# Chunk 1's sublayer ahead of chunk 0's ranks in the second FFN, and the rows of ones written in the first FFN

## What is computed

```python
def ffn(x):                 # top 2 of 8 experts, unweighted
    gamma = softmax(x @ w_router.T + b_router)
    mask = top_k(gamma, 2)  # as a 0/1 mask over 8 experts
    return einsum('bte,bteo->bto', mask, x @ w_experts.T + b_experts)
def attn(t):                # causal, 16 heads, scale 1/4
    out = softmax_causal(q @ k.T / 4) @ v
    x = out @ w_proj + b_proj + t
    return layernorm(x) * ln_gamma + ln_beta
x = x + 0.5 * ffn(ln(x))
x = x + attn(ln(x))
x = x + 0.5 * ffn(ln(x))
```

## Time and profile before

| | us |
|---|---|
| median of 3 runs | 1021.81 (1019.46 to 1022.9) |
| profiled execution, its own time | 1021.86 |
| its span, first to last instruction | 1020.1 |
| PE busy | 966.9 (95%) |
| DVE busy | 833.7 (82%) |
| ACT busy | 512.4 (50%) |
| POOL busy | 264.5 (26%) |
| granted PE clock, mean | 0.974 of 2.4 GHz |

### The profile page before, as it was taken

How to read it: one execution, slowest core, us unless ns; L and a number is a source line. 1 busy time by engine, 2 the same in 40 slices (tenths; PEclk the granted TensorE clock), 3 DMA queues, 4 the chain that set the end, 5 groups by cost and what they waited for, 6 DMA issues and landing times.

```text
span 1020.1 us, 18105 instructions
## 1 busy us (share of the span) xinstructions
PE 966.9 (95%) x5602; PEld 575.7 (56%) x5602; DVE 833.7 (82%) x2444; ACT 512.4 (50%) x1053; POOL 264.5 (26%) x289
## 2 busy tenths in 40 slices
PE   6899999999888699999999999999998899999997
PEld 5678887888665233333333333333344677777776
DVE  5677776767675999999999999999767788888775
ACT  4225434442322277777777777777774333232310
POOL 1012202221420412222122121221342443434211
PEclk9999999999996699999999999999999899999999
DMA  6201101113113412222222223322320111110001
GB/s 224 83 1 63 63 0 62 63 41 84 62 43 82 126 40 66 75 68 72 70 70 72 75 76 75 76 75 76 95 54 13 43 63 63 62 56 21 7 21 41
DMA packets 55058, 64.27 MB, mean 63 GB/s; under 512 B 13776, under 2 KB 37312, under 8 KB 54976
## 3 DMA queue, kind: packets, MB, share of 16 engines
q1 hardware_dynamic: 54384, 62.47, 21.5%
q10 hardware_dynamic: 592, 0.80, 0.2%
HBM read 41.30 MB, written 21.23 MB: 61 GB/s over the span
## 4 chain that ended last, share of the span: by engine, by line
PE 86%; DVE 8%; issue 2%; ACT 2%; DMA 1%; POOL 1%; DVEq 0%; SPq 0%; POOLq 0%; ACTq 0%
PE bank L354 39%; PE bank L1503 14%; PE bank L1330 14%; PE bank L1487 13%; PE bank L800 2%; PE bank L346 2%; DMA v_all<-L_ffn_w_experts 1%; ACT b_probs L1466 1%; DVE bank L1357 1%; DVE c_acc L999 1%; PE bank L751 1%; DVE a_acc L999 1%; DVE b_neg L1361 1%; DVE a_st L309 1%; DVE c_wins L970 0%
## 5 line engine op out<-in xcount | busy, mean ns | idle before, releaser
L1466 ACT ACTIVATE b_probs<-bank 128x512 f32<-128x512 f32 (+1 forms) x608 | 302.3, 585 | 122.2 <-PE bank L1487 121.8
L1330 PE MATMUL bank<-b_ks,b_qs 96*128 96x512 bf16 (+3 forms) x768 | 226.4, 337 | 18.5 <-DVE b_neg L1357 6.2
L1357 DVE CUSTOM_DVE_ANT_0 bank<-bank,b_below 128x384 f32<-128x384 f32 (+3 forms) x512 | 234.9, 516 | 7.7 <-PE bank L1330 6.1
L1487 PE MATMUL bank<-b_qs,b_ks 99*128 99x512 bf16 (+3 forms) x768 | 214.0, 330 | 4.7 <-ACT b_probs L1466 4.6
L354 PE MATMUL bank<-we,c_xt 128*128 128x512 f32 x768 | 190.2, 403 | 2.3 <-DVE c_acc L999 2.3
L354 PE MATMUL bank<-we,a_xt 128*128 128x512 f32 x768 | 190.5, 402 | 1.7 <-DVE a_acc L999 1.7
L1440 POOL TENSOR_SCALAR_AFFINE_SELECT b_probs<-b_probs 128x512 f32<-128x512 f32 x128 | 83.7, 654 | 327.7 <-ACT b_probs L1466 327.7
L354 PEld LDWEIGHTS bank<-we,c_xt 128*128 128x128 f32 x768 | 143.6, 191 | 34.5 <-DVE c_acc L999 2.8
L1361 DVE TENSOR_REDUCE b_neg<-bank 128x1 f32<-128x512 f32 x256 | 160.6, 679 | 3.0 <-PE bank L1330 1.6
L354 PEld LDWEIGHTS bank<-we,a_xt 128*128 128x128 f32 x768 | 143.0, 191 | 30.6 <-DVE a_acc L999 1.8
L1503 PE MATMUL bank<-b_probs,b_vs 128*32 128x512 f32 (+3 forms) x1536 | 154.9, 498 | 0.8 <-POOL b_probs L1440 0.8
(11 more groups left out here) (133 smaller groups left out, 881.1 us busy)
## 6 DMA issues: line engine op xcount, KB each, us to landing
b_qs<-q_parts SPq DMA_DIRECT2D x96, 128.0 KB, 3.0
b_ks<-k_parts SPq DMA_DIRECT2D x96, 128.0 KB, 3.1
q_parts<-a_part SPq DMA_DIRECT2D x16, 384.0 KB, 2.7
k_parts<-a_part SPq DMA_DIRECT2D x16, 384.0 KB, 2.6
att_num<-b_oev SPq DMA_DIRECT2D x64, 64.0 KB, 2.2
c_num<-att_num SPq DMA_DIRECT2D x8, 512.0 KB
c_rec<-att_rec SPq DMA_DIRECT2D x16, 256.0 KB
out<-xs SPq DMA_DIRECT2D x8, 512.0 KB, 3.1
```

The lines of the kernel that those rows point to most:

```text
L1330: last = nc.tensor.matmul(ms[bank][:, a * width:(a + 1) * width], qs[g.u][0:ROWS, c, i * P:(i + 1) * P], ks[g.u][0:ROWS, c, lo:lo + width] ...
L1357: last = dve.tensor_tensor_reduce(part, part, below[:, CH - width:CH], -1.0, 3.0e38, ALU.add, ALU.min, dst[:, a, :])
L1466: act.activation(probs[b % 4][:, heads[0]:heads[0] + hp, 0:width], es[exp_bank(g, unit)][:, 0:hp * width].rearrange("p (h w) -> p h w", w= ...
L1487: last = nc.tensor.matmul(es[exp_bank(g, unit)][:, a * width:(a + 1) * width], ks[g.u][:, c, j * P:(j + 1) * P], qs[g.u][:, c, first_q:fir ...
```

## The change

In the first FFN's last slot (c = 8) POOL now writes the rows of ones of K's buffer 1 behind the last expert bank, and K's buffer 2 and V's buffer 1 behind the last values bank, all ahead of the low parts of chunk 7. The start of attention no longer writes them. In the second FFN, DVE's block 0 of group 15 now takes `attended(2)` ahead of `split_lo(0)` and behind it chunk 1's `scale3`, `sublayer` and statistics; its block 2 takes the residual of chunk 2, `ranks(0)` and `scale(1)`. ACT's root of chunk 1's layer norm (`spread3(1)`) moves from block 9 to block 7, its `logits_out(0)` from 10 to 9, and `spread(1)` ahead of `mask_out(0, 0)`. PE's `router(0)` moves from block 9 to 8 and `turn_logits(0)` from 11 to 10.

```diff
@@ first FFN, gpsimd, slot
                 if exists(c):
                     add_tiles(c, range(TPC))
+                if isinstance(c, int) and c == NCH:
+                    pool.wait_ge(q.qk_lo, at(4 * (NCH - 1)))
+                    pool.wait_ge(q.ffn_bank, at(16 * NCH))
+                    a.ones_keys(pool, 1, 3)
+                    pool.wait_ge(q.v_bank, at(2 * NCH))
+                    a.ones_keys(pool, 2, 4)
+                    a.ones_values(pool, 1, 5)
                 if exists(c - 1):
                     low_parts(c - 1)
@@ second FFN, scalar, lead
                 if (early, block) == (0, 7):
                     split_hi(0, 0)
+                    spread3(1)
                 if (early, block) == (0, 9):
-                    spread3(1)
-                if (early, block) == (0, 10):
                     logits_out(0)
 
             a.scalar(act, lead)
+            spread(1)
             mask_out(0, 0)
-            spread(1)
             norm(1)
@@ second FFN, tensor, lead
-                if (early, block) == (0, 9):
+                if (early, block) == (0, 8):
                     router(0, 0)
-                if (early, block) == (0, 11):
+                if (early, block) == (0, 10):
                     turn_logits(0)
@@ second FFN, vector, lead
                     stats3(1)
+                    attended(2, 0, 1)
                     split_lo(0, 0)
-                    attended(2, 0, 1)
+                    scale3(1)
+                    sublayer(1)
+                    norm(1)
+                if (early, block) == (0, 2):
                     dve.wait_ge(q.resid_bias, at(2))
                     dve.sem_inc(q.apart, 1)
                     scale_tiles(resid, xs_tile(2), s.ln2[:, tiles(2), :], q.resid_ready)
-                if (early, block) == (0, 2):
                     ranks(0, 0)
-                    scale3(1)
-                    sublayer(1)
-                    norm(1)
                     scale(1)
@@ attention
-    def ones(pool, u):
-
-        if u < 2:
-            pool.memset(vs[u][:, :, :, HD:SLOT], 1.0).then_inc(vones, 1)
-            pool.wait_ge(vones, at(2 * u + 1))
+    def ones_values(pool, u, nth):
+        pool.memset(vs[u][:, :, :, HD:SLOT], 1.0).then_inc(vones, 1)
+        pool.wait_ge(vones, at(nth))
+
+    def ones_keys(pool, u, nth):
         pool.memset(ks[u][ROWS:MROWS, :, :], 1.0).then_inc(vones, 1)
-        pool.wait_ge(vones, at(min(2 * u + 2, 5)))
+        pool.wait_ge(vones, at(nth))
...
-        ones(pool, 0)
+        ones_values(pool, 0, 1)
+        ones_keys(pool, 0, 2)
...
     def gpsimd(pool, lead):
-        for u in (1, 2):
-            ones(pool, u)
-
```

More of the change, by code:

```diff
@@ L1565, in attention @@
     a.v_read, a.load, a.ready_group0, a.first_scores, a.first_reads = v_copied, load, ready_group0, first_scores, first_reads
-    a.consts = consts
+    a.consts, a.ones_keys, a.ones_values = consts, ones_keys, ones_values
     a.sync, a.gpsimd, a.scalar, a.tensor, a.vector = sync, gpsimd, scalar, tensor, vector
```

## The result

The changed kernel takes 1014.45 us (median of 4 runs, 1013.01 to 1014.85) against 1021.7 of the kernel before (4 runs, 1019.46 to 1022.9). The ratio is 0.9935, with a 95% interval of 0.9919 to 0.9951: faster by 0.65%, which is 6.6 us; the two medians lie 7.2 us apart. The forecast was 1013.3 with a range of 1011.0 to 1017.0. The profiled execution took 1014.85 with a span of 1013.1, which is 7.0 us less than before.

A forecast was written before the change was run, and what follows sets the result against it. The chain was taken as 86% PE, with two PE waits near the edits, at the starts of attention and the second FFN. 1021.86 - 3.2 - 5.4 = 1013.3 us; 8-in-10 range 1011.0 to 1017.0, own range 1012.2 to 1014.8.

The forecast's parts named there:

- Part 1: Start of attention: moving the rows-of-ones memsets frees two DVE casts, 3.40 us less, 0.17 paid elsewhere; sum -3.2.
- the 0.17 behind POOL's low parts: First FFN's last slot: chunk 7's low parts queue behind the moved memsets and delay PE's first maxima by 0.17 us.
- Rival (b): First FFN's last slot: memsets hold DVE's two-input operations, the ones' move gives only 0.1, 1016.4 us; chance 0.05.
- Part 2: Second FFN's new order: PE's stretch starts 2.78 us earlier and runs 2.72 shorter, less 0.1 for slips; -5.4.
- the 1.2 GHz level in the stretch: Second FFN, PE's 30 expert matmuls: with little idle ahead the clock holds, 6.97 us in place of 9.69.
- ranks' first wide operation waits until POOL ends, plus 0.3, then five more steps, 2.0: Second FFN, DVE: only ranks' first wide operation meets POOL's addition; mask at 784.0, 1.6 us later than before.
- PE's own end of attention: End of attention: PE's project(2) ends at 782.4, or 783.0 with the slips, then waits for the mask.
- PE's own chain is last, by 1.0: Second FFN: PE's mask-to-transpose chain ends at 792.0, the combine pair it needs at 791.0.
- (a): Second FFN: clock falls in PE's new wait for the mask, 2.7 us comes back, 1016.0; chance 0.17.
- (c): Second FFN: late denominators or missed ACT roots leave about 1 us of 5.4, 1017.7; chance 0.07.
- (d): Second FFN: mask later than its delay pays for, kernel slower, 1025 us at a mask of 793; chance 0.03.
- (e): Start of attention: clock falls later or rises sooner, about 1 us of half-speed work, 1011.8; chance 0.10.

The follow-up runs named there:

- e1: Kernel before with only the rows of ones moved to the first FFN's last slot: 1016.9 us, ratio 0.9966.
- e8: Kernel before with the rows of ones still at the start of attention, but POOL waits with them for the last step of the maxima's split: 1020.92 us, ratio 0.9994.
- e4: Changed kernel with both POOL operations of chunk 2 (bias addition and shift of x) held until the mask is there: 1012.38 us, ratio 0.9903.
- e12: Changed kernel, unedited, profiled once more; no time given, second bias 34.95 us behind chunk 0's transposes.
- e3: Changed kernel with only POOL's shift of x for chunk 2 held until chunk 0's mask is there: 1013.55 us, ratio 0.9914.
- e11: Changed kernel, unedited, profiled once more: 1016.63 us.
- e6: e4 plus the last group's four denominator DMAs issued ahead of the four numerator DMAs: 1013.05 us, ratio 0.992.
- e7: e6 plus PE turning the mask between the two halves of chunk 2's projection: 1012.34 us, ratio 0.9913.
- e2: Kernel before with only the second FFN's new order: 1017.62 us, ratio 0.9971.
- e10: Kernel before, unedited, profiled once more; no time given, second bias 39.63 us behind chunk 0's transposes.
- e9: Kernel before, unedited, profiled once more; no time given, second bias 39.09 us behind chunk 0's transposes.

## Why the prediction was right, point by point

**Part 1 (-3.2 forecast).** Right in mechanism and size. PE resumed 3.42 earlier and chunk 0's transposes were 3.5 earlier. The casts are at 0.21 and 0.22, the 0.17 behind POOL's low parts was paid, and L320 passed the memset at 0.16. e1 gives 3.5 us by time, e8 the cause. Rival (b) is out: the memset didn't hold the two-input DVE operation beside it. The Trainium skill's page "SBUF — State Buffer", section "SBUF: two separate sides", ties that case to a GpSimd operation that reads SBUF; the trace agrees on both sides (L320 0.16 beside a memset, L976 2.58 beside L485).

**Part 2 (-5.4 forecast, -3.3 measured in the profile).** The way of the gain was right: the sublayer fits beside the last products, the idle of 2.6 and 1.8 us ahead of the stretch goes, and with it the 1.2 GHz level in the stretch, -2.72 as told. The step that was mis-sized is "ranks' first wide operation waits until POOL ends, plus 0.3, then five more steps, 2.0". The mask's transpose was 21.22 - 17.24 = 4.0 later on the common scale, and so was the mask, not 1.6. Ranks took 7.2 us, where the forecast had about 4.7. I had followed what DVE's moved steps wait for, and not what they release: sublayer(1) lets POOL's L491 start, which stood at 786.90 before, behind ranks, and came at 779.37 now, in the middle of it. With both POOL operations held ranks takes 2.9 us (e4). With this one alone held, the mask's transpose comes 1.7 earlier than in the profile of after and 1.0 earlier than in e12 (e3).

The second mis-sized term is PE's own end of attention. It came 0.6 later by the forecast and 15.64 - 13.69 = 1.95 in the profile. It was not last there, since PE still waited 1.86 us for the mask; with the denominators behind it, it is what is last in e3 and e4. 0.9 of it is the clock's fall behind the transposes; the rest, 14.75 - 13.67 = 1.1, is of the order. In e11, where the clock held, the parts that I had named are there (ACT's roots ahead of block 8, a select held by DVE), but their split was not tried. The last denominators leave later with it: from the reciprocal's start to the transposes it was 22.0 in the profile, where the forecast had 20.4.

"PE's own chain is last, by 1.0" held, by 1.6, since the mask, from which that chain starts, and the denominators both slipped: the pair that PE needs was there at 789.0, and PE came to it at 790.6. The start of the stretch gained 0.6 in place of 2.8.

**Rivals.** (a) did occur, in one profile of four of the changed kernel: 1016.63, where 1016.0 was given for it at a chance of 0.17. It came behind the wait for the late mask, 2.32 us in e11; e3, e4, e6 and e7 have no such wait and no such fall, one profile each. (c) and (d) didn't occur; the landing was no worse than 1.7 us behind the last issue. (e) wasn't seen: from PE's resuming to the transposes it was 421.7 us, and 421.8 before. Its price is also added up wrong, for 1 us less would be 1012.3 and not 1011.8.

**Sum.** The forecast was 1.2 us under the median and 1.6 under the profiled execution. In that one the terms are -3.5 for -3.2, -3.3 for -5.4, and 0.15 in the rest. Part 1's small error made up for a little of part 2's, by luck. The range held the result since it was drawn wide enough for the clock and for unknown meetings of POOL and DVE; this meeting was no term in it. The own range of the forecast, up to 1014.8, holds the median by 0.35 only. With the collision counted, 2.5 us more of mask, the same working would have given a stretch 0.3 earlier in place of 2.8, and 1015.8 as the time.

## What to carry to other kernels

When a step moves forward, follow what it releases as well as what it waits for: its consumers on other engines start earlier too, and one of them can hold the step that is now critical and eat part of the gain (here a POOL addition of 2.5 us in the middle of DVE's ranks). A wait that puts such an operation behind the critical one cost nothing here (e3, e4), and the next limits can then be taken one by one (e6, e7). In this kernel the one-time fills by GpSimd belong where DVE makes no casts from SBUF to SBUF.

## What the runs showed of the hardware

- A cast of 32x128 elements took 3.22 us in place of 0.21 beside a memset of three partitions; in e8 the same cast took 0.21, with that memset starting 1.3 us after it.
- A two-input DVE operation from SBUF took 0.16 beside a memset (L320).
- DVE operations that took 0.21 to 0.42 alone lasted until 0.1 to 0.3 us behind the end of a POOL addition of 2.5 us: L976 2.58 and L978 2.52, and L979 of e2, a one-input step with a bf16 output of 96 columns, 1.84. The reduction L973 of e2 took its 0.42 beside the same addition.
- The granted clock at one place differed between executions of the same kernel. With the same 0.74 us of idle ahead and the same work, it fell to 0.50 in e10 and stayed at 1.00 in e9. Over all 14 profiles it fell in 9 (after, e2 to e6, e8, e10, e12). It fell in both orders, and what decides it in an execution stays open.
- A wait of PE for 2.32 us was followed by a fall (e11), one of 1.86 us in the profile of after was not. With the falls behind 0.74 us, the length of the idle alone doesn't decide it.
